# Third chunk's q and k products ahead of its conv, all q loads on one queue, statistics spread 8/6/18

## The reference

```python
x = x + _L0_conv_ref(_gn(x), ...)

def _L0_conv_ref(x, ...):
    residual = x
    h = relu(bn(conv1x1(x, conv1_w)))           # 512 -> 128 channels
    h = lambda_layer(h, ...)                    # 128 -> 128
    h = relu(bn(h))
    h = bn(conv1x1(h, conv3_w))                 # 128 -> 512
    return relu(h + residual)

def lambda_layer(x, ...):
    q = bn(conv1x1(x, q_w))                     # 4 heads x 16
    k = softmax(conv1x1(x, k_w), axis=1)        # 16, over the channels of each pixel's k row
    v = bn(conv1x1(x, v_w))                     # 32
    pos = 15 x 15 convolution of each v plane with emb, 16 filters
    content_lambda = einsum('bkm,bvm->bkv', k, v)
    return einsum('bhkn,bkv->bhvn', q, content_lambda) + einsum('bhkn,bkvn->bhvn', q, pos)
```

## Time and profile before

| | |
|---|---|
| Time, median of 3 runs | 4807.04 us (4805.04 to 4808.21) |
| Profiled execution: its time, its span | 4802.3 us, 4800.5 us |
| Busy share of the span: TensorE, VectorE, ScalarE, GpSimd | 92%, 58%, 49%, 20% |
| TensorE clock granted, mean | 0.959 of full |
| DMA share of 16 engines: SP's queue, ScalarE's queue | 63.8%, 16.8% |

### The profile page before, as it was taken

How to read it: one execution, slowest core, us unless ns; L and a number is a source line. 1 busy time by engine, 2 the same in 40 slices (tenths; PEclk the granted TensorE clock), 3 DMA queues, 4 the chain that set the end, 5 groups by cost and what they waited for, 6 DMA issues and landing times.

```text
span 4800.5 us, 121009 instructions
## 1 busy us (share of the span) xinstructions
PE 4394.3 (92%) x49366; PEld 2693.8 (56%) x49366; DVE 2802.7 (58%) x4631; ACT 2335.2 (49%) x2880; POOL 966.8 (20%) x529
## 2 busy tenths in 40 slices
PE   4899999999999999999999999999999999999997
PEld 2555555655565655566555555555555555555554
DVE  3465655665655655556656556656566555566564
ACT  1454445454445554455544454544555544445444
POOL 0022202122211222112222121222112221112222
PEclk8899999999999999999999999999999999999998
DMA  2688778898878897788887788987888977889876
GB/s 94 212 283 288 245 269 276 277 306 271 261 270 269 283 307 256 257 277 284 282 297 245 265 278 274 304 270 249 280 271 283 306 255 252 271 269 304 267 246 246
DMA packets 537174, 1284.17 MB, mean 268 GB/s; under 512 B 43048, under 2 KB 225324, under 8 KB 528556
## 3 DMA queue, kind: packets, MB, share of 16 engines
q1 hardware_dynamic: 456396, 992.83, 63.8%
q10 hardware_dynamic: 80352, 284.45, 16.8%
HBM read 844.79 MB, written 432.33 MB: 266 GB/s over the span
## 4 chain that ended last, share of the span: by engine, by line
PE 59%; issue 12%; DMA 9%; DVE 6%; SPq 6%; POOL 4%; ACT 3%; ACTq 2%; POOLq 0%; DVEq 0%
PE ring L526 15%; PE ring L652 13%; PE ring L507 12%; PE ring L582 8%; DMA X<-x_dram 4%; DMA q_parts<-region 3%; DVE st L892 3%; PE ring L606 2%; POOL region L1191 2%; PE ring L533 2%; PE ring L616 2%; ACTq L813 2%; PE ring L538 2%; POOL X L1198 1%; SPq L402 1%
## 5 line engine op out<-in xcount | busy, mean ns | idle before, releaser
L701 ACT COPY region<-ring 126x1024 f32<-126x1024 f32 x1120 | 1103.2, 1015 | 971.7 <-PE ring L507 958.1
L582 PE MATMUL ring<-h,w3T 128*128 128x512 f32 x2048 | 991.5, 624 | 22.9 <-ACT h L720 13.2
L526 PE MATMUL ring<-X,w1e 128*128 128x512 f32 x2048 | 909.0, 597 | 3.2 <-DVE w1e L918 3.2
L652 PE MATMUL ring<-region,V 126*32 126x128 f32 x24576 | 874.9, 286 | 34.3 <-issue 34.2
L507 PE MATMUL ring<-Qt,Ep 96*126 96x256 bf16 x5120 | 759.4, 288 | 47.7 <-ACT region L701 30.8
L652 PEld LDWEIGHTS ring<-region,V 126*32 126x32 f32 x24576 | 686.1, 115 | 196.8 <-issue 191.1
L701 DVE COPY region<-ring 126x1024 f32<-126x1024 f32 x416 | 507.0, 1219 | 439.9 <-PE ring L507 416.6
L892 DVE BATCH_NORM_STATS2 st<-X 128x6 f32<-128x512 f32 x1024 | 624.7, 678 | 196.4 <-DMA X<-x_dram 196.3
L507 PEld LDWEIGHTS ring<-Qt,Ep 96*126 96x126 bf16 x5120 | 578.5, 141 | 252.9 <-issue 160.2
L526 PEld LDWEIGHTS ring<-X,w1e 128*128 128x128 f32 x2048 | 385.0, 191 | 469.6 <-issue 466.3
L582 PEld LDWEIGHTS ring<-h,w3T 128*128 128x128 f32 x2048 | 380.0, 198 | 406.1 <-issue 374.1
(11 more groups left out here) (130 smaller groups left out, 3263.4 us busy)
## 6 DMA issues: line engine op xcount, KB each, us to landing
X<-x_dram SPq DMA_DIRECT2D x132, 2048.0 KB, 20.0
out_dram<-X SPq DMA_DIRECT2D x512, 512.0 KB, 7.9
X<-x_dram ACTq DMA_DIRECT2D x124, 2048.0 KB, 10.2
V<-v_windows SPq DMA_DIRECT2D x96, 1024.0 KB, 10.9
Qt<-q_parts SPq DMA_DIRECT2D x582, 128.0 KB, 4.1
lambda_sums<-S SPq DMA_DIRECT2D x64, 1024.0 KB, 4.9
h<-lambda_sums SPq DMA_DIRECT2D x256, 256.0 KB, 5.0
q_parts<-region SPq DMA_DIRECT2D x128, 256.0 KB, 4.2
```

The costliest lines, as they stand in the source:

```text
L526: last = nc.tensor.matmul(dst[:, hh * HALF:(hh + 1) * HALF], w1e[:, c, :], X[:, j, c, hh * HALF:(hh + 1) * HALF], start=(c == 0), stop=(c ...
L582: last = nc.tensor.matmul(dst[:, yb * HALF:(yb + 1) * HALF], w3T[:, t, :], src, start=True, stop=True)
L652: last = nc.tensor.matmul(bank_of(i)[c * DV:(c + 1) * DV, (g % 4) * P:(g % 4 + 1) * P], V[0:TROWS, VSLOT[t], xb, yb * DV:(yb + 1) * DV], W ...
L701: return engine_copy(dst, src)
```

## The change

Four things are changed:

- In the mixed list q2 and k2 stand ahead of c3, o1.0 stands between c3 and q3, and q3 and k3 follow.
- The lead begins after o3.0 (it began after o2.2): o2.3 and o3.0, then w0.0 and w0.1, o3.1, then w0.2, w0.3 and r0, o3.2, then r1, w0.4 and w0.5, o3.3, then w0.6 and w0.7. `placed` and `prior` follow from the list.
- ScalarE's `load_q` of chunk 2 goes; SP does it, directly behind store_q of chunk 2 and ahead of store_q of chunk 3. Output store 3 moves ahead of store_q of chunk 2.
- Statistics by unit 1, 2 and 3: 8, 10 and 14 before, 8, 6 and 18 after; the last two slots of unit 2 have none.

```diff
-STATS_AT = {1: (0, 0, 0, 0, 2, 2, 2, 2), 2: (1, 1, 1, 1, 0, 2, 2, 2), 3: (2, 2, 2, 2, 2, 2, 2, 0)}
+STATS_AT = {1: (0, 0, 0, 0, 2, 2, 2, 2), 2: (1, 1, 1, 1, 0, 2, 0, 0), 3: (3, 3, 2, 2, 2, 2, 2, 2)}
@@ mix_names
-    order = ["c0", "nb", "c1", "q0", "k0", "o0.0", "o0.1", "c2", "q1", "k1", "o0.2", "o0.3", "c3", "q2", "k2", "q3", "k3",
-             "o1.0", "o1.1", "o1.2", "o1.3", "cl", "o2.0", "cp", "o2.1", "o2.2", "w0.0", "o2.3", "w0.1"]
-    lead = lead_names()[2:]
-    for t in range(4):
-        order += [f"o3.{t}", lead[2 * t], lead[2 * t + 1]]
-    return order
+    order = ["c0", "nb", "c1", "q0", "k0", "o0.0", "o0.1", "c2", "q1", "k1", "o0.2", "o0.3", "q2", "k2", "c3", "o1.0",
+             "q3", "k3", "o1.1", "o1.2", "o1.3", "cl", "o2.0", "cp", "o2.1", "o2.2", "o2.3", "o3.0"]
+    lead = lead_names()
+    return order + lead[0:2] + ["o3.1"] + lead[2:5] + ["o3.2"] + lead[5:8] + ["o3.3"] + lead[8:]
@@ sync, in the loop
                 store_out(b, 2)
+                store_out(b, 3)
                 store_q(b + 1, 2)
-                store_out(b, 3)
+                load_q(b + 1, 2)
                 store_q(b + 1, 3)
                 load_q(b + 1, 3)
                 store_v(b + 1)
@@ scalar
-            def load_q(im, j):
-                act.wait_ge(q_out[j], im * 32 + 32)
-                ...
@@ scalar, in the loop
-                    if name == "k3":
-                        load_q(b + 1, 2)
```

## The result

The changed kernel takes **4962.05 us** (median of four, 4958.56 to 4973.42) against 4807.62 before: ratio 1.0325, 95% interval 1.0306 to 1.0343. It is 154 us slower where 79 were forecast. Its profiled execution took 4958.56 us and is the one read here. One execution of a kernel further down (the statistics alone) was in a slow state, at 23632 us; the ratio given there is of the other four.

A forecast was written before the change was run, and what follows sets the result against it. TensorE, busy 92%, bounds the kernel, with a loop through SP's x loads close below. Pass 143.6 + 5.0 = 148.6 us against 145.85; thirty passes 81 us, less 2, on 4802.3, plus 4.7, gives 4886 us; range 4765 to 4950.

The forecast's parts named there:

- Statistics: VectorE, units 2 and 3: four statistics move behind the second sums copy; pass 2.3 us shorter if x lands as now.
- x landing: First x chunk of the next image, loaded by SP: lands 5.0 us later, 0 at the quiet end, 9 at the slow.
- Landing of chunk 2's parts: SP's stores of chunk 2's parts: land about with the reload, at 2169.2, between ends of 2162.7 and 2172.2.
- The quiet end: Chunk 2's parts land 3.0 us after their store, at 2162.7; x then lands as now.
- rival 2: Chunk 2's parts land before 2165.8, x under 2.3 us later, gains stay; value 4750 us, chance 0.18.
- SP's chain in series: SP, from first load of chunk 2's q to load of the v windows: 21.5 to 22.2 us, as in the prologue.
- From w5.1 to c0: TensorE, from VectorE's finished copy of w5.1 to the next pass's c0: 11.46 us.
- case 1: The forecast itself: v load late on SP, x lands late; 4886 us, own range 4825 to 4980, chance 0.65.
- Lead behind o3.0 at nothing: TensorE's lead: up to 3 us idle at w0.0, adding nothing to the pass while the x loop is later.
- q2 ahead of c3: Mixed list: q2 ends 7.0 us earlier, c3 3.8 later; GpSimd's later split of chunk 3 is not felt by SP.
- Rival 3: Moving the loads costs only their issues: x 0.4 us later, pass 144.0 us, 4752 us; chance 0.07.
- Rival 4: DMA engines catch up half the shift: x 2 to 2.5 us later, no change, 4800 to 4812 us; chance 0.10.

The follow-up runs named there:

- the later reload: Changed kernel with ScalarE's reload of X for chunk 3 issued behind k3 instead of right behind c3; 4964.35 us against 4814.71 for the kernel before, ratio 1.0317.
- the one-wait kernel: Changed kernel with SP's store of chunk 3's parts ahead of its loads of chunk 2's q; 4872.99 us against 4809.12 for the kernel before, ratio 1.0129.
- both with the v store first: Statistics-alone kernel with SP's v store ahead of its chunk 3 q load, 4977.16 us; the same plus ScalarE's chunk 2 q load behind the copy of cl, 4972.45 us.
- x later: Statistics-alone kernel with the load of the last v windows ahead of the four x loads on SP; 4945.68 us against 4804.12 for the kernel before, ratio 1.0295.

## Why the prediction was right or wrong

The direction was right and so was the way: SP waits, the v load is late, x is late, the pass follows. The size was not: 4886 was forecast with an upper end of 4950, and 4962 was measured. What failed are three terms of the sum, each too small: the first x landing (111.4 us after c0 in the working, 112.82 measured), because chunk 2's parts land later than it took them to; VectorE's chain from there to w5.1 (25.7 us, measured 26.66); and the way from w5.1 to c0 (11.46, measured 11.81).

- **The gaps at cp and at the content product** go, as forecast: of these two waits of the earlier trace rows only 0.4 us at cp, once in the run, are left in after.
- **Statistics.** Forecast as 2.3 us a pass where x lands as now; alone they gave 1.15. With them alone VectorE's chain from the x landing to w5.1 became 1.80 us shorter (26.28 against 28.08), and the way from w5.1 to c0 0.71 longer (12.45 against 11.74). By the fit, unit 0's loop ends there in the same place as x's (144.8 and 144.7), so part of the gain is cut off. In the changed kernel, where x is late, VectorE's chain from the x landing to the end of w5.1's copy took 139.48 - 112.82 = 26.66, against 28.08 before. The sum of rows had 25.7. **This term was 0.96 too small**: I gave 0.5 for what VectorE waits for, and the mean over the passes is 1.7: 0.75 for the second sums, 0.62 for position tiles, 0.30 for x. In the sample pass above the wait for the second sums alone is 1.32 us (in the sample pass of before those two copies had statistics between them).
- **Landing of chunk 2's parts.** Forecast at 57.9 us after c0 (2169.2 - 2111.3), measured 59.17. **This landing was taken 1.27 us too early**, and it is the larger part of what x came late. The choice of the middle, beside the reload, was right: the parts land 0.3 us behind the reload, and the later reload shows it the other way round (52.83). The size was not: the 10.2 us of the earlier trace rows are the median of the reloads of all four chunks. Those of chunks 0 and 1 take 8 to 9 us; that of chunk 3 takes 11.6 in the mean, before as after, which the trace of before already had. The quiet end, on which rival 2 stood, did not occur in the changed kernel.
- **SP's chain in series.** 21.5 us from the prologue; 80.53 - 59.17 = 21.36 in the loop. Right.
- **x landing.** Forecast 5.0 later, measured 6.57, with the v load 6.84 later. **The step "a little may be, so I take 5.0"** had no row behind it and took 0.7 off the 5.7; the DMA engines gave back 0.27. Together with the later parts, which are the larger share, x came at 112.82 where the working has 2217.7 - 2111.3 + 5.0 = 111.4: 1.4 too early.
- **From w5.1 to c0.** 11.46 in the sample pass of the earlier trace rows; in the mean 11.74 before and 11.81 after. A single pass was taken for the mean, 0.35 us too short.
- **Sum.** 1.42 + 0.96 + 0.35 = 2.7 us a pass, and 30 times that, 81 us, stands against the 76 by which the forecast was low. None of the three is large; all three went the same way, and thirty passes multiply them. The range was made from the x landing alone (3 to 8 us) and left the other two at their middle values, and I cut its upper end at 4950 although case 1's own range went to 4980. With x at the measured 112.82 and the rest as forecast the working gives 112.82 + 37.2 = 150.0 us a pass and some 4930 us, inside the range; the other two terms carry the time out of it.
- **Lead behind o3.0 at nothing.** Right in the sum and wrong as a price. In the changed kernel it lies beside the later x loop, as the sentence in the prediction had it; alone it costs 84 us. Its wait for q loads, forecast at up to 3 us in a pass, is 53.7 us in 30.
- **q2 ahead of c3.** GpSimd's split "which SP does not feel": true in the changed kernel, where SP is late by its own wait (it stores chunk 3's parts right behind its loads), not by itself. With the loads on ScalarE it costs x 2.6 us, and 69 us.
- **Rival 3 and the skill's rule.** The runs speak for SP's wait and against a price of the issues alone: the v load moved by 6.84 us for 3.8 us of issues, and the one-wait kernel, with the same issues, gave back 3.7 of it. Taken one after the other, the list makes 2.18 of the 6.84 (73.69 to 75.87), the loads on SP 0.98 (to 76.85), and the wait in series 3.68 (to 80.53). The Trainium skill, "DMA: Bandwidth & Descriptors", section "Issuing engines are not separate DMA queues", counts only the sequencer's time for the issue as what a second issuing engine saves. Here the second engine also took a wait for a landing out of the way of everything queued behind it, and of the price of the loads that was the larger part.
- **Rival 4**, half of it caught up, falls with 0.27 of 6.84.

The signs that the prediction named came in the order forecast, each somewhat later: the load of the v windows near 80 (80.53), x near 111 (112.82), w5.1 near 137 (139.48), and TensorE idle in front of w0.0 and of unit 3's last tile.

What stays open: TensorE's idle time without a releaser (below); what part the granted clock has in the loss of four kernels (0.942 to 0.946 in the mean for the loads alone, both with the v store first, and x later; 0.952 to 0.967 in the other nine traces); and how much of SP's two waits is the reload's. Moving the reload shifted its weight from one store to the other, and no run here has the reload away from both.

## What to carry to other kernels

Moving a transfer to another engine's queue moves its wait too: before you count issues, write down what stands behind the wait in the queue that takes it, and follow that to the last transfer in it. When two loops close a pass within a fraction of a us of each other, an edit that shortens one gains only up to the other, and a list that is moved to help one must be priced on both. Take the terms of a sum that is multiplied by the passes from means over many of them, and let every term move in the range, not the largest alone. Take a landing time from transfers of the same place in the pass, not from a median over several places.

## What the runs showed of the hardware that I had not expected

- **Issues took over twice as long beside SP's store of v.** Six q loads took ScalarE 3.84 us, and 8.96 us while SP issued the store of v and, behind it, its own six loads. Two engines that issue at the same time are not enough for it: in the earlier trace rows ScalarE's six loads and SP's six overlap, from 2171.31 to 2173.06, and take 3.84 and 3.96 us. What in the store of v does it is not shown.
- **A store beside a 2 MB load takes two to three times as long to land.** Chunk 2's second store is issued 49.2 us after c0 in the changed kernel and lands at 59.17, with the reload and two output stores in flight; with the reload away it is issued at 49.1 and lands at 52.83.
- **TensorE idles inside runs of matmuls, with no releaser in the trace** ("issue"): 54.4 and 53.0 us at lines 652 and 616 in the kernel with the statistics alone, 15.4 and 117.4 us at the matching lines 654 and 618 in the one with x later. Its cause is open.
